# One more set of single transfers in each head, and the diagonals moved from ScalarE to VectorE

## The reference

```python
def _L0_gnn_ref(h, adj, W, a):                # h: 8 x 1024 x 128
    Wh = h @ W
    e = (Wh @ a[:D]) + swapaxes(Wh @ a[D:], 1, 2)
    e = where(e > 0, e, 0.2 * e)
    e = where(adj > 0, e, -inf)
    return elu(softmax(e) @ Wh)

def _L0_ffn_ref(x, Wq_pk, pk_keys, Wq, keys_table, values_table, Wo):
    q = (x @ Wq).reshape(b, n, 8, 128) * 128 ** -0.5
    kv_scores, ind = _pk(x, Wq_pk, pk_keys)   # 16 chosen rows of 16384 for each token and head
    k = einsum('bnhk,bnhkd->bnhd', kv_scores, keys_table[ind])
    v = einsum('bnhk,bnhkd->bnhd', kv_scores, values_table[ind])
    sim = where(causal, einsum('bihd,bjhd->bhij', q, k), neg)
    out = einsum('bhij,bjhd->bhid', softmax(sim), v)
    return out.reshape(b, n, 1024) @ Wo

x = x + _L0_gnn_ref(layernorm(x), adj, W, a)
x = x + _L0_ffn_ref(layernorm(x), ...)
```

## Time and profile before

| | |
|---|---|
| median of 3 runs | 10074.95 us |
| span of the profiled execution | 10059.9 us |
| one head in the middle of the span (kT copy of unit 0 to the next) | 155.05 us |
| GpSimd busy | 7544.0 us, 75% |
| VectorE busy | 6956.2 us, 69% |
| ScalarE busy (DMA issue not counted) | 3087.9 us, 31% |
| TensorE matmul busy | 5726.9 us, 57% |
| DMA | 109 GB/s |

### The profile page before, as it was taken

One profiled execution on the slowest core, in us unless ns is written; L12 is line 12 of the kernel. 1 busy time (PEld: TensorE's weight loads), 2 busy tenths in 40 slices (PEclk: granted clock), 3 DMA queues, 4 the chain that ended last, 5 costly groups with the idle time before them and its releaser, 6 DMA issues.

```text
span 10059.9 us, 190416 instructions
## 1 busy us (share of the span) xinstructions
PE 5726.9 (57%) x23108; PEld 4551.2 (45%) x23108; DVE 6956.2 (69%) x42844; ACT 3087.9 (31%) x9770; POOL 7544.0 (75%) x7957
## 2 busy tenths in 40 slices
PE   5655555555555555555555555555555555555555
PEld 4544444444444444444444444444444444444444
DVE  8876667666666677676776666767667676666664
ACT  4333233233333333333333333333333332322222
POOL 5777777777777777777777777777777777777776
PEclk7877777777777777777777777777777777777777
DMA  3333343333433334333343333333333333333333
GB/s 109 105 109 109 109 114 109 109 109 109 113 109 109 109 109 113 109 109 109 109 113 109 109 109 109 113 109 109 109 111 111 110 109 109 109 111 109 109 109 100
DMA packets 503669, 1100.92 MB, mean 109 GB/s; under 512 B 196992, under 2 KB 246912, under 8 KB 502144
## 3 DMA queue, kind: packets, MB, share of 16 engines
q0 software_dynamic: 381120, 1041.22, 36.4%
q1 hardware_dynamic: 71488, 31.70, 1.3%
q10 hardware_dynamic: 49664, 16.42, 0.8%
HBM read 1084.36 MB, written 4.19 MB: 108 GB/s over the span
## 4 chain that ended last, share of the span: by engine, by line
POOL 73%; issue 24%; DVE 1%; PE 1%; POOLq 0%; DMA 0%; ACT 0%; ACTq 0%; SPq 0%; DVEq 0%
POOL ring L353 73%; DVE hot L1013 0%; DMA wo<-in_Wo 0%; POOLq L369 0%; PE ps_o L724 0%; ACTq L492 0%; POOLq L367 0%; DVE ps_v L935 0%; DMA ring<-in_table,idx 0%; PE ps_p L610 0%; PE ps_p L614 0%; DVE nmax L1064 0%; PE ps_s L748 0%; POOLq L368 0%; DVE cand L987 0%
## 5 line engine op out<-in xcount | busy, mean ns | idle before, releaser
L353 POOL DMA_INDIRECT ring<-in_table,idx x7940 | 7542.5, 950 | 2491.2 <-issue 2420.6
L671 PE MATMUL ps_w<-ring,diag 128*128 128x256 f32 x8192 | 2151.7, 423 | 13.0 <-issue 8.7
L715 PE MATMUL ps_p<-ident,prob 128*128 128x128 f32 x2304 | 564.7, 400 | 2304.0 <-ACT prob L453 2296.3
L671 PEld LDWEIGHTS ps_w<-ring,diag 128*128 128x128 f32 x8192 | 1740.6, 218 | 297.1 <-issue 19.7
L1013 DVE SCALAR_TENSOR_TENSOR hot<-rank,posf,cand 128x54 f32<-128x54 f32 x8192 | 1654.5, 271 | 0.3
L715 PEld LDWEIGHTS ps_p<-ident,prob 128*128 128x128 f32 x2304 | 395.1, 202 | 2501.0 <-ACT prob L453 1600.2
L932 DVE TENSOR_SCALAR ps_v<-ring,wgt 128x256 f32<-128x256 f32 x512 | 248.4, 485 | 1837.0 <-DMA ring<-in_table,idx 1836.8
L935 DVE SCALAR_TENSOR_TENSOR ps_v<-ring,wgt,ps_v 128x256 f32<-128x256 f32 x3072 | 1478.9, 481 | 19.6
L444 ACT ACTIVATE diag<-ident,wgt 128x128 f32<-128x128 f32 x4096 | 1251.8, 391 | 0.0
L453 ACT ACTIVATE prob<-ps_s,nmax 128x128 f32<-128x128 f32 (+7 forms) x512 | 378.1, 738 | 2300.8 <-issue 2259.6
L724 PEld LDWEIGHTS ps_o<-probT,kv 128*128 128x128 f32 x4608 | 986.7, 304 | 144.9 <-ACT probT L461 81.6
(11 more groups left out here) (119 smaller groups left out, 8141.2 us busy)
## 6 DMA issues: line engine op xcount, KB each, us to landing
far<-in_table SPq DMA_DIRECT2D x16352, 1.0 KB
far<-in_table ACTq DMA_DIRECT2D x15904, 1.0 KB
ring<-in_table,idx POOLq DMA_INDIRECT x7940
xin<-in_x SPq DMA_DIRECT2D x8, 512.0 KB
mask<-in_adj SPq DMA_DIRECT2D x1, 4096.0 KB, 15.9
out_x<-acc SPq DMA_DIRECT2D x64, 64.0 KB
far_row<-far_at SPq DMA_DIRECT2D x128, 0.5 KB
far_row<-far_at ACTq DMA_DIRECT2D x124, 0.5 KB
```

The source lines that it names most:

```text
L353: pool.indirect_dma_start(out=ring[:, t % RING, k, :], out_offset=None, in_=table, in_offset=bass.IndirectOffsetOnAxis(ap=idx[:, t, k:k + ...
L671: ins = nc.tensor.matmul(pw_ps, diag[:, k, :], ring[:, t % RING, k, :], start=(k == 0), stop=(k == PE_ROWS - 1))
L715: ins = nc.tensor.transpose(ps_p[:, c, (j % 4) * P:(j % 4 + 1) * P], prob[:, j * P:(j + 1) * P], ident[:])
```

## The change

There are now five sets: units 1, 6, 0, 4 and 3 (`SETS`, with positions 0 to 4). SyncE loads the units 1 and 6 and the first 64 rows of unit 3; ScalarE loads the units 0 and 4 and the last 64 rows of unit 3. That is 320 single transfers a head on each, and 123 gathers. ScalarE's rows are spread over its units by the table `NEAR_PARTS`: lists of 20 and 20 rows in units 1, 2, 5 and 6, of 24 and 24 in units 3 and 7, and one of 32 in units 4 and 0. Of each unit, 8 transfers still come ahead of `oT` and `qT`, and the second list is loaded behind the rest of the first. In head 0 ScalarE now loads in its units 4 to 7, and SyncE loads the sets of units 0, 1, half of 3, and 6. At the turn of a batch the order of SyncE's input load and stores among the sets is other than before.

The diagonals leave ScalarE. VectorE makes all eight in one TENSOR_TENSOR of 128x1024, right behind `sum_rows`, and TensorE waits for one count where it waited for eight.

```diff
-FAR = (3, 7)
-NEAR = (0, 4)
-SETS = FAR + NEAR
-NEAR_UNITS = 4
+SETS = (1, 6, 0, 4, 3)
+SP_ORDER = (0, 4, 1)
+SP_STOP = {0: P, 4: 64, 1: P}
+SP_FIRST_ORDER = (2, 0, 4, 1)
+NEAR_BEGIN = {1: 2, 5: 3}
+NEAR_PARTS = {1: (2, 0, (20, 20)), 2: (2, 40, (20, 20)), 3: (2, 80, (24, 24)), 4: (4, 64, (32,)),
+              5: (3, 0, (20, 20)), 6: (3, 40, (20, 20)), 7: (3, 80, (24, 24)), 0: (4, 96, (32,))}
+FIRST_PARTS = (4, 5, 6, 7)
...
-            def far_sets(n, sets, final=False):
-                for i in sets:
-                    if i < last_set:
-                        far_begin(n, i + 1)
-                    elif not final:
-                        far_begin(n + 1, 0)
+            def far_sets(n, order, follows):
+                for j, i in enumerate(order):
+                    if j + 1 < len(order):
+                        far_begin(n, order[j + 1])
+                    elif follows is not None:
+                        far_begin(n + 1, follows)
                     far_fetch(n, i)
...
-            def diagonals(n, t):
-
-                act.wait_ge(pw_mm, n * UNITS + t)
-                act.wait_ge(wgt_ready, n * UNITS + t + 1)
-                for k in range(PE_ROWS):
-                    nc.scalar.mul(diag[:, k, :], ident[:], wgt[:, t, k:k + 1]).then_inc(diag_ready, 1)
...
-                    if t < UNITS - 1:
-                        if not first or t + 1 > SUMMED:
-                            diagonals(n, t + 1)
-                    elif ahead:
-                        diagonals(n + 1, 0)
-                    fetch = not first and (ahead or t == 0)
+                    fetch = t in FIRST_PARTS if first else ahead or t == 0
                     if fetch:
-                        near = len(FAR) + (t - 1) % UNITS // NEAR_UNITS
-                        part = (t - 1) % NEAR_UNITS
-                        at = near_load(n + 1 if t else n, near, part)
-                        near_rows(near, part, at, range(0, HIDDEN))
+                        near, start, loads = NEAR_PARTS[t]
+                        at = near_load(n + 1 if t else n, near, start, loads[0], True)
+                        near_rows(near, start, at[:HIDDEN])
...
                     if fetch:
-                        near_rows(near, part, at, range(HIDDEN, LOADED))
+                        near_rows(near, start + HIDDEN, at[HIDDEN:])
+                        start += loads[0]
+                        for rows in loads[1:]:
+                            near_rows(near, start, near_load(n + 1 if t else n, near, start, rows, False))
+                            start += rows
...
-                pe.wait_ge(diag_ready, (u + 1) * PE_ROWS)
+                pe.wait_ge(diag_ready, u + 1)
...
+            def diagonals(n, t):
+
+                dve.wait_ge(pw_mm, n * UNITS + t)
+                dve.wait_ge(wgt_ready, n * UNITS + t + 1)
+                nc.vector.tensor_tensor(diag[:], ident[:].unsqueeze(1).broadcast_to([P, PE_ROWS, P]),
+                                        wgt[:, t, 0:PE_ROWS].unsqueeze(2).broadcast_to([P, PE_ROWS, P]),
+                                        ALU.mult).then_inc(diag_ready, 1)
...
                         c = choose_sums(n, t, a_unit, c, add_row)
                         sum_rows(n, t)
+                        diagonals(n if t < UNITS - 1 else n + 1, (t + 1) % UNITS)
                         choose_rows(t, a_unit, c)
```

More of the change, by code:

```diff
@@ L287, in far_fetch @@
                     sp.sem_inc(sp_mark, 1)
-                for q in range(0, stop, LOADED):
+                for q in range(0, SP_STOP.get(i, P), LOADED):
                     _, at = nc.values_load_multi_w_load_instructions(
@@ L309, in turn @@
+            def turn(b, more):
+                n = (b + 1) * HEADS
+                far_begin(n, SP_ORDER[1])
+                far_fetch(n, SP_ORDER[0])
+                if more:
+                    load(b + 2)
+                far_begin(n, SP_ORDER[2])
+                far_fetch(n, SP_ORDER[1])
+                far_begin(n + 1, SP_ORDER[0])
                 stores(b)
-                far_sets((b + 1) * HEADS, range(last_set, last_set + 1))
+                far_fetch(n, SP_ORDER[2])
             load(1)
-            far_begin(1, last_set + 1)
@@ L314, in _ @@
[L314 to L321, removed]
+            far_begin(1, SP_FIRST_ORDER[0])
+            far_sets(1, SP_FIRST_ORDER, SP_ORDER[0])
             with sp.Fori(2, HEADS) as h:
-                far_sets(h, range(len(FAR)))
+                far_sets(h, SP_ORDER, SP_ORDER[0])
@@ L324, in _ @@
             with sp.Fori(0, BATCH - 2) as b:
-                load(b + 2)
-                turn(b)
+                turn(b, True)
                 with sp.Fori(1, HEADS) as h:
-                    far_sets((b + 1) * HEADS + h, range(len(FAR)))
-            turn(BATCH - 2)
+                    far_sets((b + 1) * HEADS + h, SP_ORDER, SP_ORDER[0])
+            turn(BATCH - 2, False)
             with sp.Fori(1, HEADS - 1) as h:
-                far_sets((BATCH - 1) * HEADS + h, range(len(FAR)))
-            far_sets(BATCH * HEADS - 1, range(len(FAR)), True)
+                far_sets((BATCH - 1) * HEADS + h, SP_ORDER, SP_ORDER[0])
@@ L333, in _ @@
+            far_sets(BATCH * HEADS - 1, SP_ORDER, None)
             stores(BATCH - 1)
@@ L473, in near_begin, with near_load @@
                     act.dma_start(far_row[0:1, i, :], far_at[:, i:i + 1]).then_inc(far_row_dma[i], 16)
-            def near_load(n, i, part):
-                if part in (0, NEAR_UNITS - 1):
+            def near_load(n, i, q, rows, waits):
+                if waits:
                     act.wait_ge(far_row_dma[i], n * 16)
                     act.sem_inc(act_mark, 1)
-                    act.wait_ge(rows_summed, (n - 1) * UNITS + SETS[i] + 1)
-                    act.sem_inc(act_mark, 1)
-                q = part * LOADED
+                    if not (isinstance(n, int) and n == 1):
+                        act.wait_ge(rows_summed, (n - 1) * UNITS + SETS[i] + 1)
+                        act.sem_inc(act_mark, 1)
                 _, at = nc.values_load_multi_w_load_instructions(
-                    far_row[0:1, i, q:q + LOADED], engines=[mybir.EngineType.Activation],
+                    far_row[0:1, i, q:q + rows], engines=[mybir.EngineType.Activation],
                     min_val=0, max_val=(HEADS * NUM_KV - 1) * KV_BYTES,
@@ L487, in near_load, with near_rows @@
                 return at
[L489 to L492, removed]
+            def near_rows(i, q, at):
+                for j, offset in enumerate(at):
+                    act.dma_start(far[q + j:q + j + 1, i, :].bitcast(U8), table_bytes[bass.ds(offset, KV_BYTES)]) \
                         .then_inc(far_dma[i], 16)
@@ L520, in _ @@
             choose_begin(0, UNITS, 0)
-            diagonals(0, SUMMED)
             query_weights(1, 1)
@@ L537, in head @@
                         graph_keep(b + 1, h, g)
-                    if ahead and t in (1, 1 + NEAR_UNITS) and not first:
-                        near_begin(n + 1, len(FAR) + t // NEAR_UNITS)
+                    if ahead and t in NEAR_BEGIN and not (first and t not in FIRST_PARTS):
+                        near_begin(n + 1, NEAR_BEGIN[t])
                     if ahead:
@@ L1059, in _ @@
                 weights(it, it)
+                if it >= LEAD - 1:
+                    diagonals(0, it + 1 - LEAD)
             clear_steps()
@@ L1109, in head @@
                         sum_rows(n, t)
+                        if t < UNITS - 1:
+                            diagonals(n, t + 1)
                     if graph:
```

7 lines of the change are left out of this document (1 added, 6 removed).

## The result

The kernel after takes 11,173.35 us (median of 4 runs, 11,170.83 to 11,183.24) against 10,074.03 us before on the same chip. The ratio is 1.109, with a 95% interval of 1.108 to 1.111. The forecast was 11,050 us in 10,560 to 11,520, so the sign and the engine that became the bound were right, and the time was 1.1% too low. The profiled execution of after spans 11,169.9 us.

What follows compares the result with a forecast made beforehand. GpSimd bound the kernel before; ScalarE was to become the bound at 169.8 us a head against GpSimd's 154.4. Start 347, heads 10,507, projections 81 and end 103 gave 11,038, plus 15: 11,050 us, range 10,560 to 11,520.

Steps and rivals of the forecast that it cites:

- the 139.1 us of head 1: Head 1 before the change, where GpSimd has a lead: ScalarE itself was claimed to set its 139.1 us.
- Transfers, 64 x 0.31 = 19.8: ScalarE's stream: 64 more transfers a head at 0.31 us, +19.8 us a head, with nothing to hide them.
- Lists, +10.4: ScalarE's stream: second address lists in six units, first ones shortened; +10.4 us a head, the middle of +6.1 and +14.6.
- Diagonals, -1.2: ScalarE: of 19.6 us a head of datapath work removed, at most the handing over was counted as gain, 1.2 us.
- VectorE, +1.2: VectorE's new instruction, 1.2 us a unit, was to be seen only in unit 0: +1.2 us a head.
- SyncE, "I put this at nothing": SyncE's queue: 24.5 us more transfers a head, claimed covered by its waits for choices, 24 us twice a head: cost nothing.
- the base head: Head 1 of the kernel before, 139.1 us, to which the forecast added the change's costs to get 169.8 us a head.
- 0.5 for it and `oT`: ScalarE's copies `oT` and `qT`, reached earlier, may wait for TensorE: 0 to some 3 us a head, taken as 0.5.
- the 11,038 of the sum: Whole kernel's forecast span: head 1's start near 347, heads 10,507, six projections 81, last head and end 103 us.
- The 15 us that I added for the time: Whole kernel: median time before lay 15 us above the profiled span, so 15 us were added to the summed span.
- B: Rival: GpSimd stays the bound, VectorE's new instruction stretching its gathers by 0.44 us a unit; 10,220 us, chance 0.10.
- C: Rival: the diagonals' 19.6 us a head do come off ScalarE's stream, so the kernel gets faster; 9,996 us, chance 0.05.

Runs made afterwards that it cites:

- the run with thirty fewer: The kernel after with 30 of ScalarE's 320 transfers a head left out, the last five behind each of six second lists: 10,821.15 us, ratio 1.0757.
- the sets alone: The kernel after with the diagonals back on ScalarE as eight instructions a unit, the five sets kept: 11,072.93 us, ratio 1.1009 to the kernel before.

## Why the prediction was right, and where its sizes were off

**The bound.** Right: the 139.1 us of head 1 were ScalarE's, and what came on top went into the head at nearly full price. Beside the waits that I read in the earlier trace rows that head has 2.2 us for `oT` and 0.6 for `qT`, too little to change this.

**Transfers, 64 x 0.31 = 19.8.** Right: 0.30 to 0.32 us each by the run with thirty fewer, so 19 to 20.5, and nothing hid them.

**Lists, +10.4.** Too dear. A list of 20 took 1.48 us and one of 24 1.72: the price goes nearly with the number, near the low end. Leaving out the six second lists took 11.1 us off their units; the shorter first lists give 4 x 0.67 + 2 x 0.42 = 3.5 back. Net +7.6. The Trainium skill's floor (DMA: Bandwidth & Descriptors, Latency and other measured facts) gave 1.56 and 1.75 as estimates, 0.03 to 0.08 above the rows; the rows decide.

**Diagonals, -1.2, and VectorE, +1.2.** The reason was right: with the diagonals back on ScalarE the time fell. Their removal gave 1.0 us a head in six units. VectorE's instruction takes the 1.2 us forecast, and unit 0 got 1.4 longer by it.

**SyncE, "I put this at nothing".** This step failed in its reasoning. I priced SyncE's transfers against its waits for choices, and not what waits for SyncE. The cover that I asked for is there: SyncE still waits 39 us a head for choices.

```profile
SPq L281 <- DVE idx L1017: 2492.0, 64, 51.1
```

What failed is the order in its queue. Unit 4's list hangs on addresses that SyncE sends behind a whole set, and that set stands behind one of these waits (for the choice of unit 1 of the next head, which is made at 4905.3, just ahead of the rows below). In after, SyncE's loop's turn and sending, and ScalarE's unit 4, show it:

```profile
4908.30 48.37 SPq L298 DMA_DIRECT2D far<-in_table  x128
4959.61 0.50 SPq L283 DMA_DIRECT2D far_row<-far_at  x1
```

```profile
4961.89 0.25 ACT L442 COPY kT<-ps_t 128x128 f32<-128x128 f32 x1
4964.98 2.65 ACTq L485 DMA_DIRECT2D far<-in_table  x8
```

3.1 us pass between keys and transfers where units without that wait need 1.4 and a longer list 0.7 more. This is some 1 us in each head of the batches 1 to 6, and it is a second bound close behind: when ScalarE was made 11 or 9 us faster, 4.8 and 3.6 came back there.

**The head.** It came to 169.8 us in head 1, where the base head was taken. That this is the sum's figure to the tenth is luck: the lists were 2.8 us too dear, and about as much that I had left out stands against them. Of that, 0.8 us is the wait for `qT`, 1.3 longer where I took 0.5 for it and `oT`; the rest no row shows singly. SyncE's wait is not in it: unit 4 of head 1 takes 17.9 us, and 18.3 before the change. The heads of batches 1 to 6, the turns left out, take 170.8 to 173.7 us, 172.0 on average, and those of batch 0 170.4. Of the difference 0.8 us is in unit 4 (18.7 to 19.5) and 1.3 in unit 7 (32.0 to 33.3), and this second part is something that the base head lacks. ScalarE at the end of head 1 and of a head in the middle:

```profile
513.09 14.72 ACTq L485 DMA_DIRECT2D far<-in_table  x40
530.98 0.30 ACT L437 COPY wq_cur<-wq 128x128 f32 x1 [17.69 <-issue]
...
5025.97 14.80 ACTq L485 DMA_DIRECT2D far<-in_table  x40
5043.79 1.28 ACT L437 ACT_TABLE_LOAD   x1 [17.61 <-issue]
```

48 heads load a table of 1.28 us there, also before the change (the load at 5096.16 in the earlier trace rows is of that line): 61 us, hidden then behind GpSimd. Why some of these heads take 171 us and others 173 stays open; the 2 us spread over the units 4 to 7.

**The whole.** The span came out 132 us above the 11,038 of the sum. The 15 us that I added for the time have no ground: in every execution on record with both, the time is about 2 us above the span (11,171.68 for 11,169.9), so the profiled execution before was a faster one than the median. (1) Head 1 starts at 370.3 and not at 347: +23. ScalarE in unit 4 of head 0:

```profile
254.47 0.26 ACT L442 COPY kT<-ps_t 128x128 f32<-128x128 f32 x1
284.62 2.71 ACTq L485 DMA_DIRECT2D far<-in_table  x8
```

I priced the wait for SyncE's addresses there at 14 us. It was some 28 (30.1 less a list), and 26.7 went when ScalarE sent for them itself. SyncE's first set starts at 231.2 us there and not at 211.2, since it first sends for the addresses of unit 1 and waits for that choice: again what stands ahead in its queue. (2) The 48 heads from 1392.7 to 9750.6 us took 126 us more than forecast, projections included: 61 are the table loads, 32 the turns (19 us each, table loads apart, where I took 13.6), and the remaining 33 lie in the 36 heads between the turns, 0.9 us each. (3) The last eight heads took 24 us less: without graph work a head saves 7 to 8 us, the table load among them, and not 3. (4) Batch 0's heads and the last head add 4 and 3.

**The rivals.** B's hold is real at 0.42 us a unit, and in after, where GpSimd waits once in nearly every head, it is hidden, as the forecast said: 3.4 us a head beside some 16 of idle time. C fell with the sets alone. What C wanted, a gain, came from another division of the rows and not from the diagonals.

## What to carry to other kernels

An engine's queue has three prices: its datapath, its sequencer's stream (transfers and lists that it issues), and what others get from it and when; the second and the third can be the bound while the busy share falls. Before work is moved onto an engine that "waits anyway", look who waits for what it sends and what stands ahead of that in its queue; idle time elsewhere in the queue does not cover it. Price the queue from the period of its loop and not from one long row. Take the base stretch from the same part of the program as the heads that it stands for: a head of batch 0 lacked a table load that 48 others have.

## What the runs showed of the hardware that I had not expected

- A list of addresses costs ScalarE 1.48, 1.72 and 2.13 us for 20, 24 and 32 words: nearly a straight line, 0.054 us a word above 0.4 us.
- Moving one input of a VectorE instruction from SBUF to PSUM left its 1.22 us as they were and took 1.8% off the kernel: the gathers' mean fell from 977 to 953 ns, 191 us for 7940 of them.
- The end of a loop's body costs SyncE some 3 us between its last transfer and the next instruction that the trace shows (4956.67 to 4959.61 in after).
